# Layer 2 of a four-layer kernel in a new order, and pauses between the scatters of layer 0

## The chip, the cores and the metric

One core of one Trainium2 chip runs the whole program in one launch. The metric is the device time of an execution in microseconds.

## The reference

The input `x` is 16 batches of 128 tokens of 256 values. Four layers follow, each an attention and an FFN, added to `x` behind a gate `tanh(g)`. Only two parts matter here.

Layer 0's FFN is a shared FFN of 704 hidden values for all tokens and eight experts of 176, of which each token takes its best two:

```python
s1 = xf @ shared_fc1.T; s2 = xf @ shared_fc2.T
shared = silu(s1) * s2 @ shared_proj.T
top_p, top_i = top_k(softmax(xf @ gate_w.T), 2)
y = sum over the two experts of top_p * expert(xf) + sigmoid(xf @ shared_gate_w.T) * shared
```

Layer 2 is an attention to a context (16 heads of 16, scores clipped to +-50) and an FFN with values rounded to 8 bits and ternary weights:

```python
probs = softmax(clip(mask(clip(q @ k.T / 4))))
delta = rs * ((probs @ v) @ Wo.T + bo)
x = x + tanh(g_xattn[2]) * ((delta - mean) / sqrt(var + 1e-5) * gamma + beta)
act_quant(a) = round(a * 127 / max|a|) / (127 / max|a|)
gate = silu(act_quant(n) @ quant(w_gate).T); up = act_quant(n) @ quant(w_up).T    # n = layernorm(x)
x = x + tanh(g_ffn[2]) * (act_quant(gate * up) @ quant(w_down).T)
```

## The kernel before, in words

Each engine has a queue of instructions written out by hand: `pe_program`, `dve_program`, `act_program`, `pool_program`, `sp_program` of each stage. An engine runs its queue in order; a wait holds everything behind it. Marks are semaphores: `.up()` counts one, `.at(n)` waits for the n-th.

**Layer 0's FFN (`l0_ffn`).** The shared FFN is cut into 24 up blocks and 24 down blocks, v = 0 to 23 (four groups of batches, six pieces of the hidden width). For each: `pe_up` (L1052, eight matmuls), ScalarE's tanh (L1243), two multiplications on VectorE (L1187, L1189), `pe_down` (L1064). Blocks up to 17 (`LATE` is 18) run before the experts, the rest after them. When the routing is known (L1175), GpSimd scatters the tokens' rows to DRAM, 16 DMAs for each of the two choices (`pool_scatter`, L1265), and then gathers the first eight tiles' expert weights (L1485); the last two of these wait for up block 17. SyncE loads the sorted rows (L1523) when all scatters have landed. Then 39 tiles of 128 rows go through the experts (`pe_tile_up`, L1329, and so on).

**Layer 2 (`layer_2`).** A loop over 16 batches works on several at once: in iteration i the keys or queries of a pair are made two pairs ahead, the scores and exponentials of batch i, the attention result of batch i - 2 = y (sum and FFN up projection), and the FFN's hidden values and down projection of batch i - 3 = f. A batch's 16 heads are two units of eight, u = 2b and 2b + 1. Per unit: scores (L2653, eight matmuls), exponential on ScalarE (L3054), clip on VectorE (L2849), weighing of the values (`pe_weigh`, L2670), and `dve_normalise`: transpose (L2857), reciprocal (L2859), multiply (L2861), transpose back (L2866). The weights V hold a column of ones, so the sum of the probabilities comes with the product. Both units use the same 256 columns of one PSUM bank, `av_bank`; the output projection (`pe_project_out`, L2679, L2681) writes the same columns too.

On VectorE then: statistics of the projection (`dve_delta_stats`, L2871 to L2875), a scaling (L2879) and the sum into `x` (L2883), the FFN's layer norm statistics (L178 to L182), the rounding of the normalised values (`dve_ffn_quantise`, L2895 to L2904), and in `dve_ffn_gate` (L2914 to L2928) the product of gate and up, its maximum, three one-column steps for the scale and the rounding of 832 columns. The hidden values are transposed (`pe_turn_hq`, L2712), copied by ScalarE (L3078, L3079) and go through the down projection (L2719). GpSimd makes the root of every variance (`ln_root`, L190; `pool_delta_root`, L3174), splits projections into bf16 parts (L3165, L3169), makes scales (L3181, L3182, L3189), adds the FFN output (L3193), and in every odd iteration up to the ninth norms a pair of batches that comes three pairs later (L190 twice, L3147 twice, L3160 twice).

Functions named `ahead` are the start of layer 3, put into the last iterations.

## Time and profile before

| | |
|---|---|
| Runs | 1975.53 us median of 3 (1969.91 to 1983.47) |
| Profiled execution | 1976.86 us, span 1975.5 us |
| Busy in the span | PE 87%, DVE 67%, ACT 48%, POOL 40% |
| Mean granted clock of TensorE | 0.944 |

The profile is of one execution. PE is TensorE's matmuls, PEld its weight loads, DVE VectorE, ACT ScalarE, POOL GpSimd, SP SyncE. Times in it count from the start of the span. A row of a timeline merges like instructions that follow each other (x8 is eight of them); what stands in brackets is how long the engine sat idle before it and what released it. A window's row gives the busy time of each engine in a stretch.

### The profile page before, as it was taken

The page shows a single profiled execution, that of the slowest core. Times are in us where ns is not written, and L with a number is a line of the kernel's source. Part 1 is how long each engine was busy: PE and PEld are TensorE (multiplying, and loading weights), DVE is VectorE, ACT ScalarE, POOL GpSimd, SP SyncE. Part 2 cuts the span into 40 slices and gives each one's busy share as a digit, 9 for nine tenths or more (in the row PEclk, how much of TensorE's full clock was granted, in tenths as well). Part 3 has the DMA queues.
Part 4 walks back from the last instruction along what each step waited for, and adds up shares of the span by engine and source line. Part 5 has one row for each costly group of instructions (what it writes and reads, how often), then busy time and mean ns, then how long its engine had stood idle before and what let it go on. Part 6 is the DMA issues. An engine that isn't in the chain of part 4 may idle for free.

```text
span 1975.5 us, 35976 instructions
## 1 busy us (share of the span) xinstructions
PE 1726.9 (87%) x12221; PEld 1186.7 (60%) x12221; DVE 1330.4 (67%) x4195; ACT 942.1 (48%) x2227; POOL 790.8 (40%) x957
## 2 busy tenths in 40 slices
PE   6888888959897898998896787788999999988998
PEld 2444444636665777777685555455777777766445
DVE  8888873613356887887747888864576676666446
ACT  2666664203323777777644555323444444443352
POOL 3333321264664566564525454211124334433340
PEclk7999999979998999999998899788999999999899
DMA  4444422146963343443123443009100000030767
GB/s 109 102 121 101 95 55 71 36 164 218 299 182 86 82 93 78 87 92 78 32 77 95 145 125 87 18 1 308 46 18 36 32 8 4 13 97 15 232 213 306
DMA packets 180437, 200.41 MB, mean 101 GB/s; under 512 B 86500, under 2 KB 150129, under 8 KB 176928
## 3 DMA queue, kind: packets, MB, share of 16 engines
q1 hardware_dynamic: 161920, 155.92, 29.0%
q0 software_dynamic: 15168, 41.54, 6.2%
q8 instruction: 99, 1.62, 0.4%
q10 hardware_dynamic: 3168, 0.66, 0.2%
q14 instruction: 82, 0.67, 0.1%
HBM read 131.88 MB, written 75.44 MB: 105 GB/s over the span
## 4 chain that ended last, share of the span: by engine, by line
PE 51%; DVE 20%; ACT 10%; issue 7%; POOL 4%; DMA 3%; another core or an unknown queue 2%; ACTq 1%; SPq 1%; DVEq 0%; POOLq 0%
PE psum L3392 3%; PE psum L1052 3%; PE psum L389 3%; PE psum L3466 3%; PE psum L1329 2%; DVE sbuf L539 2%; PE psum L3441 2%; PE psum L352 2%; ACT sbuf L3829 2%; PE psum L3459 2%; PE psum L2278 2%; PE psum L1348 2%; PE psum L1064 2%; PE psum L1764 1%
## 5 line engine op out<-in xcount | busy, mean ns | idle before, releaser
L539 DVE TENSOR_REDUCE sbuf<-psum 128x2 f32<-128x512 f32 x256 | 164.8, 685 | 34.7 <-PE psum L352 33.7
L190 POOL TENSOR_TENSOR sbuf<-sbuf 128x1 f32<-128x1 f32 x128 | 73.5, 576 | 273.4 <-DVE sbuf L182 273.1
L2013 ACT ACTIVATE sbuf<-psum 128x512 f32<-128x512 f32 x256 | 138.4, 594 | 71.6 <-PE psum L1764 67.1
L3829 ACT ACTIVATE sbuf<-psum,sbuf 128x128 f32<-128x128 f32 x256 | 113.7, 455 | 89.2 <-DVE sbuf L3641 89.1
L681 ACT ACTIVATE sbuf<-psum 128x1024 f32<-128x1024 f32 x128 | 130.4, 1021 | 37.5 <-PE psum L374 30.0
L3921 POOL DMA_INDIRECT l_slot_inputs<-sbuf x96 | 97.3, 1014 | 100.7 <-DVE sbuf L3712 75.7
L3466 PE MATMUL psum<-sbuf 128*128 128x256 f32 x512 | 123.8, 385 | 4.9 <-DVE sbuf L3659 4.9
L3392 PE MATMUL psum<-sbuf 128*128 128x256 f32 x512 | 119.4, 388 | 0.8 <-ACT sbuf L3793 0.8
L352 PE MATMUL psum<-sbuf 112*128 112x256 bf16 x512 | 104.0, 288 | 13.1 <-DVE sbuf L539 7.8
L1889 DVE CUSTOM_DVE_ANT_0 sbuf<-psum,sbuf 128x128 f32<-128x128 f32 x512 | 112.5, 284 | 0.5 <-PE psum L1743 0.5
L3392 PEld LDWEIGHTS psum<-sbuf 128*128 128x128 f32 x512 | 98.7, 195 | 21.5 <-issue 8.8
L3466 PEld LDWEIGHTS psum<-sbuf 128*128 128x128 f32 x512 | 93.6, 193 | 16.1 <-issue 5.8
L1897 DVE TENSOR_REDUCE sbuf<-psum 128x8 f32<-128x1024 f32 x64 | 77.5, 1211 | 31.4 <-PE psum L1755 31.3
L352 PEld LDWEIGHTS psum<-sbuf 112*128 112x128 bf16 x512 | 41.6, 102 | 91.6 <-DVE sbuf L539 53.0
L1052 PE MATMUL psum<-sbuf 128*128 128x512 f32 (+1 forms) x192 | 88.0, 602 | 0.0
L3599 DVE COPY sbuf<-psum 128x1024 f32<-128x1024 f32 x32 | 39.2, 1224 | 65.0 <-ACT sbuf L3800 44.8
L2005 ACT ACTIVATE sbuf<-sbuf 128x128 f32<-128x128 f32 x256 | 81.4, 398 | 0.0
L3837 ACT ACTIVATE sbuf<-psum 128x512 f32<-128x512 f32 x64 | 38.4, 600 | 84.4 <-PE psum L3449 84.0
L374 PE MATMUL psum<-sbuf 128*128 128x512 bf16 x256 | 78.1, 387 | 0.3 <-ACT sbuf L681 0.2
L3459 PE MATMUL psum<-sbuf 128*128 128x512 f32 x128 | 69.3, 623 | 9.8 <-ACT sbuf L3837 9.8
L3441 PEld LDWEIGHTS psum<-sbuf 128*128 128x128 f32 x512 | 65.8, 195 | 17.3 <-issue 15.1
L1764 PE MATMUL psum<-sbuf 128*128 128x128 f32 x512 | 70.5, 281 | 5.2 <-ACT sbuf L2013 5.0
(436 smaller groups left out, 4501.5 us busy)
## 6 DMA issues: line engine op xcount, KB each, us to landing
l_pair_outputs<-sbuf SPq DMA_DIRECT2D x24, 512.0 KB, 7.0
sbuf<-in_l_gu_pairs SPq DMA_DIRECT2D x32, 384.0 KB, 8.6
sbuf<-l_pair_outputs SPq DMA_DIRECT2D x16, 768.0 KB, 15.9
sbuf<-l_q_parts SPq DMA_DIRECT2D x16, 384.0 KB
l_q_parts<-sbuf SPq DMA_DIRECT2D x64, 96.0 KB, 2.3
sbuf<-l_q_parts SPq DMA_DIRECT2D x32, 192.0 KB
l_k_parts<-sbuf SPq DMA_DIRECT2D x64, 96.0 KB, 2.2
sbuf<-l_k_parts SPq DMA_DIRECT2D x32, 192.0 KB
```

The source lines that it names most:

```text
L352: last = pe.matmul(score_bank[v % 2][:, j * T0:(j + 1) * T0], q3[0:STACK + 48, h, c * P:(c + 1) * P], k3[0:STACK + 48, h // 4, :], start=T ...
L539: dve.tensor_reduce(top3[:, 2 * hp:2 * hp + 2, c], score_bank[v % 2].rearrange("p (j t) -> p j t", j=2), AXX, ALU.max, negate=True).then_i ...
L681: act.activation(e_t[u % 12], shift_bank[u % 2], ACT.Exp).then_inc(*exped.up())
L1052: last = pe.matmul(up_bank[v % 2][0:M, n * BANK:(n + 1) * BANK], wn[:, k, fs], xt_t[blk][:, k, :], start=(k == 0), stop=(k == KD - 1))
L1889: last = dve.tensor_tensor_reduce(d_t[n % 3][:, head], self_bank[:, head], mask, -1.0, -LOWEST, ALU.add, ALU.min, mx[:, j:j + 1])
L2013: act.activation(e_t[i % 4][:, h * BANK:(h + 1) * BANK], turn_bank[:, h * BANK:(h + 1) * BANK], ACT.Exp).then_inc(*exped.up())
L3392: last = pe.matmul(q_bank[:, j * N:(j + 1) * N], w.wq[:, k, (4 * g + j) * P:(4 * g + j + 1) * P], xt_t[pair % 2][:, k, :], start=(k == 0), ...
L3441: last = pe.matmul(score_bank[:, j * P:(j + 1) * P], q[:, 4 * g + j, i * P:(i + 1) * P], kT_t[b % 3][:, g * P:(g + 1) * P], start=True, st ...
L3459: pe.matmul(av_bank, v_t[b % 3][:, g * P:(g + 1) * P], eT_t[u % 2], start=True, stop=True).then_inc(*valued.up())
L3466: last = pe.matmul(out_bank[:, 0:D], o_t[b % 2][:, h * P:(h + 1) * P], w.wo[:, h, :], start=(h == 0), stop=(h == H3 - 1))
L3829: last = act.activation(e_t[u % 3][:, j * P:(j + 1) * P], score_bank[:, j * P:(j + 1) * P], ACT.Exp, bias=mt[:, j:j + 1], scale=rq[:, lo + ...
L3921: pool.indirect_dma_start(out=route.x_slots[:, :], out_offset=bass.IndirectOffsetOnAxis(ap=route.slot[b][:, k:k + 1], axis=0), in_=xr_t[b ...
```

## The change

In layer 2:

- Both units of a batch are weighed in one go (16 matmuls over all 512 columns of the bank) and normalised in one go; the order of the heads in the packed result changes, and with it the rows of the output weights, which are laid out on the host (`by_group`).
- The order of the queues changes. The output projection of batch i - 1 comes late in iteration i instead of at the head of iteration i + 1. VectorE begins with the delta statistics; the clip, the attention sum and the FFN statistics follow, and only then the gate.
- The rounding of the hidden values moves from VectorE to ScalarE (`act_round_h`), in front of ScalarE's copies of the transposed values.
- The epsilon of each layer norm is no longer added by VectorE but by GpSimd, in front of the root.

In layer 0 GpSimd waits before every fourth scatter (but the first) for one more up block, 11 to 17.

```diff
+def ln_stats_only(m, src, n, var_ready, ring):
+    dve, chain, s = m.nc.vector, m.chain, ring[n % len(ring)]
+    dve.bn_stats(s[:, 0:6], src).then_inc(*chain.up())
+    dve.wait_ge(*chain.now())
+    dve.bn_aggr(s[:, 6:8], s[:, 0:6]).then_inc(*var_ready.up())
+
+def ln_root_of_variance(m, n, var_ready, eps_added, rstd_ready, ring):
+    pool, s = m.nc.gpsimd, ring[n % len(ring)]
+    pool.wait_ge(*var_ready.at(n + 1))
+    pool.tensor_scalar(s[:, 8:9], s[:, 7:8], EPS_LN, None, ALU.add).then_inc(*eps_added.up())
+    pool.wait_ge(*eps_added.now())
+    pool.tensor_tensor(s[:, 8:9], s[:, 8:9], m.half_neg, ALU.pow).then_inc(*rstd_ready.up())
...
             for b in range(NB):
+                if b % 4 == 0 and (k or b):
+                    pool.wait_ge(*upped.at(LATE - 7 + 4 * k + b // 4))
                 pool_scatter(b, k)
...
+    def pe_weigh(b):
+        pe.wait_ge(*clipped.at(2 * b + 2))
+        pe.wait_ge(*v_ready.at(b + 1))
+        if b:
             pe.wait_ge(*x_mid.at(b))
...
     def pe_project_out(b):
-        pe.wait_ge(*normed.at(2 * b + 2))
-        pe.wait_ge(*av_read.at(min(2 * b + 3, 2 * NB)))
+        pe.wait_ge(*normed.at(b + 1))
...
         for i in range(NB):                       # pe_program
             f, y, paired = i - 3, i - 2, made_in(i) < 2 * NPAIR
-            if y >= 0:
-                pe_project_out(y)
...
-            if f >= 0:
-                pe_turn_hq(f)
             if i + 2 < NB:
                 pe_values(i + 2)
             if i:
-                pe_weigh(2 * i - 1)
+                pe_weigh(i - 1)
+            if f >= 0:
+                pe_turn_hq(f)
+            if y >= 0:
+                pe_turn_xq(y)
             if f >= 0:
                 pe_down(f)
-            pe_weigh(2 * i)
-            if y >= 0:
-                pe_turn_xq(y)
             if i + 1 < NB:
                 pe_scores(2 * i + 2)
+            if i:
+                pe_project_out(i - 1)
             if y >= 0:
                 pe_up(y)
...
-        dve.tensor_scalar(c(9), c(8), c(5), 127.0, ALU.mult, ALU.mult).then_inc(*chain.up())
-        dve.wait_ge(*chain.now())
-        dve.tensor_scalar(h, h, c(9), ROUND, ALU.mult, ALU.add).then_inc(*h_round.up())
+        dve.tensor_scalar(c(9), c(8), c(5), 127.0, ALU.mult, ALU.mult).then_inc(*h_scaled.up())
...
         for i in range(NB):                       # dve_program
             f, y = i - 3, i - 2
-            if i % 2 == 1:
-                dve_clip(2 * i)
+            if y >= 0:
+                dve_delta_stats(y)
+            dve_clip(2 * i)
+            if y >= 0:
+                dve_add_attention(y)
+                dve_ffn_stats(y)
             if f >= 0:
                 dve_ffn_gate(f)
             if y >= 0:
-                dve_delta_stats(y)
-            if i % 2 == 0:
-                dve_clip(2 * i)
-            if y >= 0:
-                dve_add_attention(y)
-                dve_ffn_stats(y)
+                dve_ffn_quantise(y)
             if i:
-                dve_normalise(2 * i - 1)
-            if y >= 0:
-                dve_ffn_quantise(y)
+                dve_normalise(i - 1)
             dve_clip(2 * i + 1)
-            dve_normalise(2 * i)
...
+    def act_round_h(f):
+        act.wait_ge(*h_scaled.at(f + 1))
+        act.activation(h_t[f % 2], h_t[f % 2], ACT.Identity, bias=plus_round, scale=s_t[f % 3][:, 9:10]).then_inc(*h_round.up())
...
     def pool_delta_root(b):
-        s = y_t[b % 2][:, 8:9]
+        s = y_t[b % 2]
         pool.wait_ge(*y_var.at(b + 1))
-        pool.tensor_tensor(s, s, m.half_neg, ALU.pow).then_inc(*y_rstd.up())
+        pool.tensor_scalar(s[:, 8:9], s[:, 7:8], EPS_LN, None, ALU.add).then_inc(*eps_added.up())
+        pool.wait_ge(*eps_added.now())
+        pool.tensor_tensor(s[:, 8:9], s[:, 8:9], m.half_neg, ALU.pow).then_inc(*y_rstd.up())
```

## Rows read from the trace of the kernel before

**Rows 1.** Page, part 4, then the chain from 380 to 470 us: start, length, what.

```profile
PE 51%; DVE 20%; ACT 10%; issue 7%; POOL 4%; DMA 3%; another core or an unknown queue 2%; ACTq 1%; SPq 1%; DVEq 0%; POOLq 0%
...
403.03 17.91 another core or an unknown queue
...
420.99 19.62 another core or an unknown queue
```

**Rows 2.** Timeline of PE, 380 to 480 us: start, length, line, operation, forms, idle before.

```profile
404.54 3.60 PE L1052 MATMUL psum<-sbuf 128*128 128x512 f32 x8
...
409.70 3.60 PE L1052 MATMUL psum<-sbuf 128*128 128x512 f32 x8
...
455.85 1.45 PE L1329 MATMUL psum<-sbuf 128*128 128x352 f32 x4 [0.26 <-ACT sbuf L1441]
```

**Rows 3.** Timeline of POOL from 150 us on and from 405 us on.

```profile
387.14 1.21 POOL L1265 DMA_INDIRECT l_slot_inputs<-sbuf  x1 [33.19 <-DVE sbuf L1175]
...
428.31 1.01 POOL L1485 DMA_INDIRECT sbuf<-in_l_expert_rows,sbuf  x1 [0.30 <-issue]
```

**Rows 4.** Windows of layer 0: length; busy PE, PEld, DVE, ACT, POOL; clock; DMA; GB/s.

```profile
435.00:440.00 5.00, 0.00 (x0) 0.00 (x0) 0.00 (x0) 0.00 (x0) 0.55 (x1) 0.50 0.98 381
```

**Rows 5.** Windows, two batches of layer 2, same columns.

```profile
1152.95:1180.57 27.62, 21.58 (x185) 14.82 (x185) 24.97 (x67) 16.33 (x27) 15.33 (x22) 1.00 0.47 126
```

**Rows 6.** Timeline of DVE, 1152 to 1181 us.

```profile
1169.71 1.02 DVE L2914 SCALAR_TENSOR_TENSOR sbuf<-sbuf,psum 128x832 f32<-128x832 f32 x1
...
1173.71 0.77 DVE L2928 TENSOR_SCALAR sbuf<-sbuf 128x832 f32<-128x832 f32 x1
1174.40 0.42 DVE L2871 BATCH_NORM_STATS2 sbuf<-psum 128x6 f32<-128x256 f32 x1
...
1175.14 0.68 DVE L2849 TENSOR_SCALAR sbuf<-sbuf 128x1024 f32<-128x1024 f32 x1
1175.74 0.49 DVE L2879 SCALAR_TENSOR_TENSOR psum<-psum,sbuf 128x256 f32<-128x256 f32 x1
1176.36 0.48 DVE L2883 SCALAR_TENSOR_TENSOR sbuf<-psum,sbuf 128x256 f32<-128x256 f32 x1
...
1177.69 0.45 DVE L2857 STREAM_TRANSPOSE sbuf<-psum 128x256 f32<-128x256 f32 x1
...
1178.98 0.38 DVE L2895 TENSOR_REDUCE sbuf<-sbuf 128x1 f32<-128x256 f32 x1
```

**Rows 7.** Timeline of ACT, 1152 to 1181 us.

```profile
1161.69 0.90 ACT L3078 ACTIVATE sbuf<-psum,sbuf 128x768 bf16<-128x768 f32 x1
1162.49 0.35 ACT L3079 ACTIVATE sbuf<-psum,sbuf 64x128 bf16<-64x128 f32 x1
```

**Rows 8.** Timeline of PE, 1150 to 1200 us.

```profile
1155.46 0.69 PE L2679 MATMUL psum<-sbuf 1*128 1x256 f32 x2
1156.09 1.13 PE L2681 MATMUL psum<-sbuf 128*128 128x256 f32 x4
...
1158.78 0.61 PE L2653 MATMUL psum<-sbuf 96*128 96x128 bf16 x8
1160.67 0.98 PE L2712 MATMUL psum<-sbuf 128*128 128x128 f32 x7 [1.27 <-DVE sbuf L2928]
...
1163.23 1.06 PE L2719 MATMUL psum<-sbuf 128*128 128x256 bf16 x7
```

**Rows 9.** Timeline of POOL, 1152 to 1181 us.

```profile
1153.52 0.34 POOL L3182 TENSOR_SCALAR sbuf<-sbuf 128x1 f32<-128x1 f32 x1
...
1169.12 0.55 POOL L190 TENSOR_TENSOR sbuf<-sbuf 128x1 f32<-128x1 f32 x1 [1.29 <-DVE sbuf L182]
...
1170.40 2.44 POOL L3147 TENSOR_SCALAR sbuf<-sbuf 128x256 f32<-128x256 f32 x2
1172.80 1.23 POOL L3160 TENSOR_TENSOR sbuf<-sbuf 128x256 f32<-128x256 f32 x2
1175.31 0.94 POOL L3174 TENSOR_TENSOR sbuf<-sbuf 128x1 f32<-128x1 f32 x1 [1.27 <-DVE sbuf L2875]
```

105 lines of the change are left out of this document (49 added, 56 removed).

## The prediction

> **What bounds the kernel now.** I read the page for its share of busy time first, then the chain of waits for two stretches, then each engine's timeline there. The diff touches two places that have nothing to do with each other: the scatters of layer 0 and the loop of layer 2.
>
> In layer 0 the chain shows one odd thing [rows 1]: from 403.03 to 420.94 and from 420.99 to 440.61 us the path is "another core or an unknown queue", 37.5 us in which no engine is the cause; the page gives this item 2% of the whole span, so there is no second such place. The timelines say what it is. TensorE finishes up block 14 at 404.54 + 3.60 = 408.14 and block 15 at 409.70 + 3.60 = 413.3 [rows 2]. ScalarE's tanh of block 14 waits for nothing else that is open, yet starts at about 420.96, the end of the first piece in the chain, and that of block 15 at 440.63, the end of the second. TensorE's signal for finished work arrives 12.8 and 27.3 us late. During all this GpSimd issues 32 scatters with no pause (387.14 to 428.31, one every 1.29 us) and then, still with no pause, weight gathers [rows 3]. The experts' first projection starts only at 455.85 [rows 2], while their input rows and weights have been on their way since 428 to 430.
>
> In layer 2 two batches take 27.62 us, 13.81 each, with VectorE busy 24.97 of it, TensorE 21.58, ScalarE 16.33, GpSimd 15.33, TensorE's clock at 1.00 [rows 5]. VectorE is the bound: its queue has nearly no hole, and TensorE waits for it before the transposes of the hidden values (1.27 us [rows 8]).
>
> **The change part by part, layer 0.** The new waits let the scatters go four at a time: the first four at once, each further four when up block 11, 12, ... 17 is done. Four scatters take 4 x 1.29 = 5.15 us; TensorE does one up and one down block in 409.70 - 404.54 = 5.16 us [rows 2]. So if signals come in time the waits cost 0.1 us each. Block 17 would be done at 413.3 + 2 x 5.3 = 423.9, the last four scatters end at 429.0 instead of 428.3: +0.7 us. Behind GpSimd's waits are queued the gathers of the expert weights; behind the last scatter SyncE's loads of the rows. Nobody else uses GpSimd here.
>
> What they can buy: signals are late only inside this stream of 38 DMA issues in a row. Later gathers and stores, and layer 3's scatters, show no such piece (the 2% are used up). A pause could let the signal pass; the trace has no pause in the stretch, so nothing shows it. Bounds: 0 gained, or all of it. If all, the shared blocks end near 428 and the experts' start is set by their data: two gathers are issued by 431.6; all six and the first rows, some 4.5 MB, need 12 us at the 381 GB/s of [rows 4]. A start is possible between 434 and 443; the first pair needs a third of the data, so I take 437: 455.85 - 437 = **18.8 us gained**, between 13 and 22.
>
> Beside this a rule of the Trainium skill. By the row, the signal of block 14 is acted on 12.8 us after the last matmul's modelled end. "TensorE: Matmul & The Clock Gate", section "The mechanism", says that matmuls end in strict order and that one increment on the last is sound; it knows no lateness, and by it alone ScalarE would have started at 408. The row decides.
>
> **Layer 2, what VectorE loses.** Per batch: the rounding, 1174.40 - 1173.71 = 0.69 us [rows 6]; the epsilon after the delta statistics, of 0.74 us (1174.40 to 1175.14) about 0.18 (its own 0.07 and the wait for the aggregation, estimated), since the next instruction no longer waits for that; as much after the FFN statistics and half a time two in the norm statistics: 0.6 in all. One normalised unit takes 1.29 us (1177.69 to 1178.98), two 2.6; one double one I put at 1.9 (a transpose of 128x512 for 0.45, estimated at 0.72; reciprocal 0.24; multiply 0.45; transpose 0.45): 0.7 saved. Together 2.0 us of 13.8. ScalarE gains one pass over 832 columns, about 0.9 us (768 columns take 0.90 [rows 7]), and has 5 us free per batch. GpSimd gains three or four additions of one column. No row has one; 0.2 below (a free-running one) and 0.6 above (0.34 for a like instruction [rows 9] and its wait). I take 0.38, nearest to the 0.34.
>
> **What is late next.** Fewer VectorE cycles help only if VectorE stays the bound, and the new order closes a loop. Delta statistics of a batch now head VectorE's iteration, and wait for an output projection that TensorE runs after the down projection and the scores. The gate is behind the attention sum. So, from one end of a projection to the next: signal 0.05; delta statistics 0.56; clip 0.60 (1175.14 to 1175.74); scale 0.62 with its wait (to 1176.36); attention sum and FFN statistics 1.33 - 0.25 = 1.08 (1176.36 to 1177.69 less the epsilon); gate down to its scale 3.95 (1169.71 to just before 1173.71) [rows 6]; ScalarE's rounding 0.95; seven transposes 1.04; ScalarE's two copies 1.19; down 1.0; scores 0.58; projection 1.76 (1155.46 to 1157.22) [rows 7, 8]. Sum **13.4 us**, against 13.81 now. Of VectorE's 2.0 us only 0.4 arrives; the rest turns into VectorE waiting for the projection. TensorE, 10.8 us of work per batch [rows 5], fits in.
>
> **GpSimd's pair work.** In odd iterations up to the ninth it does, for a later pair: two roots, 1170.40 - 1169.12 = 1.28 us, now 2.05 with two additions; the norm of two batches 2.44; beta 1.23 [rows 9]. This is ahead of the next batch's delta root in its queue. Now this costs nothing: VectorE's gate (4 us) runs between, and GpSimd idles 1.27 us before that root at 1175.31. In the new order that cover is gone: the delta statistics come right after the projection. GpSimd starts the block when its addition of the FFN output is done, about 0.47 (ScalarE's scaling of 256 columns, between its 0.35 and 0.90 [rows 7]) + 0.7 (GpSimd's 0.62, half of beta, and its start) + 0.1 = 1.3 us after the down projection, which is 1.0 us before the projection's end T. It ends the block at T - 1.0 + 5.7 = T + 4.7, the root with its addition is there at T + 5.7; VectorE needs it at T + 1.83. So 3.9 us are lost once in two iterations (3.2 to 4.7 for the bounds of the addition). Two batches: 2 x 13.4 + 3.9 = 30.7 against 27.6, +3.1. It happens at iterations 1, 3, 5, 7, 9; the first lies in the start-up, where VectorE is full of weight rounding: 4 x 3.1 = +12.4. After iteration 9 the 0.4 of a batch come back, about -1; TensorE, with holes of 4 us, may be granted less than 1.00 for a while, +2. Layer 2: **+13 us**, bounds -2 and +20.
>
> A rule of the Trainium skill here: VectorE's multiply and GpSimd collide. "SBUF — State Buffer", section "Who interferes with whom", calls the shared port pair an exclusive lock. By it the bigger multiply, if it meets the norm block, would wait out one of its instructions (1.2 us); it stands in VectorE's spare time by the sum above, so I leave it at nothing.
>
> **Sum.** 1976.9 (the profiled execution; its span is 1975.5) - 18.8 + 13 = 1971; that execution is 1.3 above the median, so 1970 us.
>
> **Rivals.** *(1) The GpSimd block is hidden and the loop is shorter than summed*, because the projection overlaps more or roots come earlier: layer 2 gains 0.4 to 1.5 us in each of 13 batches, -5 to -20. For it: VectorE does lose 2.0 us. Against it: the queue order, in the diff. With layer 0's gain 1937 to 1952. *(2) Slower: the signals stay late.* Then GpSimd itself waits for the late signal, which it did not before, and scatters, row loads and gathers, all queued behind, move with it. Last scatter: issued after block 17's signal, about 441 + 5 instead of 428, experts' data some 8 us later, start near 461: +5. Decisive is whether the four-wise pause lets the signals through. 1976.9 - 1.3 + 13 + 5 = 1994, to 2000. For it: the second late signal came at 440.61, 12 us after the last scatter [rows 1, 3], so the end of the scatters alone did not free it. Against it: less is queued if scatters stop early. *(3) The stall belongs to ScalarE*: it is not GpSimd's stream that holds it but something of its own that comes late either way. Layer 0 then gives 0: 1989. By the Trainium skill's "Runtime: NRT & Kernel Launch", section "Instruction fetch mechanics", an engine's code comes in blocks over its own DMA queue and is mostly hidden; no row here shows ScalarE short of code.
>
> **Chances.** Forecast 0.44 (1960 to 1982); (1) 0.25; (2) 0.18; (3) 0.13. The measurement of this kernel tells about 1% (20 us) from no change. Faster by over 1% needs both (1) and the gain of layer 0, or the forecast's lower edge: 0.28. Slower by over 1%: most of (2) and the upper edge of (3): 0.19. Within 1%: 0.53. The range, to hold it 8 times in 10, leaves out the lower half of (1) and the end of (2): 1948 to 1996.
>
> **What would show it.** In layer 0: no piece of an unknown queue in the chain, tanh of blocks 14 to 17 about 5.2 us apart, gaps of 0.1 to 0.4 us after every fourth scatter, the experts' first projection near 437. In layer 2: two batches in about 30.7 us, 13.4 and 17.3 in turn; VectorE's attention sum waiting for GpSimd's root in even iterations and GpSimd without idle time before it; VectorE busy about 21 us per two batches; ScalarE's rounding followed at once by the transposes. I am wrong if the period falls under 13 us or the root is never waited for, or if the late signals are still there.

## The result, and the profile after

The changed kernel takes 2004.16 us (median of 4 runs, 1996.22 to 2008.68) against 1974.36 (4 runs, 1969.91 to 1983.47) for the kernel before on the same chip: ratio 1.0133, 95% interval 1.0102 to 1.0164. It is slower by 1.3%; I had forecast 1970, with a range of 1948 to 1996. The profiled execution of after took 2008.68 us, its span is 2007.3, so it stands 31.8 us above the profiled execution of before.

Where the 31.8 us arise, read from the start times of the same line in both traces: the experts' last down projection of layer 0 starts 7.6 us earlier than before (557.5 against 565.1), the first scores of layer 2 start 2.4 us earlier, layer 3's first projection of its loop starts 27.3 us later (1317.5 against 1290.2), the end is 31.8 later. Layer 0 gained, and 34 us were lost from the entry of layer 2 on.

Page of after, part 1:

```profile
PE 1736.1 (86%) x12191; PEld 1195.5 (60%) x12221; DVE 1296.8 (65%) x4068; ACT 958.4 (48%) x2243; POOL 799.1 (40%) x1005
```

**Layer 0.** Timeline of POOL: the scatter behind the only late signal that is left, and the last scatter.

```profile
419.31 0.97 POOL L1282 DMA_INDIRECT l_slot_inputs<-sbuf  x1 [2.90 <-remote]
...
433.36 0.97 POOL L1282 DMA_INDIRECT l_slot_inputs<-sbuf  x1 [0.30 <-issue]
```

Timeline of ACT and then of PE in the same stretch:

```profile
410.80 0.60 ACT L1260 ACTIVATE sbuf<-psum 128x512 f32<-128x512 f32 x1 [4.56 <-PE psum L1069]
418.56 0.60 ACT L1260 ACTIVATE sbuf<-psum 128x512 f32<-128x512 f32 x1 [7.17 <-remote]
```

```profile
440.36 1.12 PE L1336 MATMUL psum<-sbuf 128*128 128x128 f32 x4 [9.87 <-issue]
444.08 2.69 PE L1348 MATMUL psum<-sbuf 128*128 128x352 f32 x4 [2.60 <-issue]
```

Of the two late pieces of 17.91 and 19.62 us [rows 1] one is left, of 7.17 us with the tanh's own regular wait of 4.56 in it. GpSimd's next group of scatters waited 2.90 us for it, TensorE had no hole there; the experts' first up projection starts at 444.08 instead of 455.85 [rows 2].

**Layer 2.** Window of two batches, with the columns of [rows 5]:

```profile
1153.86:1189.26 35.40, 25.80 (x186) 17.47 (x186) 21.42 (x52) 18.41 (x29) 16.56 (x28) 0.84 0.37 97
```

VectorE does 21.42 us of work where it did 24.97 [rows 5], and the two batches take 35.40 us where they took 27.62. TensorE has no more to compute, but is busy 25.80 us instead of 21.58: the granted clock has gone from 1.00 to 0.84. The timelines of VectorE, GpSimd, ScalarE and TensorE say how:

```profile
1161.25 0.43 DVE L2882 BATCH_NORM_STATS2 sbuf<-psum 128x6 f32<-128x256 f32 x1 [5.83 <-PE psum L2696]
...
1175.85 0.43 DVE L2882 BATCH_NORM_STATS2 sbuf<-psum 128x6 f32<-128x256 f32 x1 [1.69 <-PE psum L2696]
...
1181.50 0.48 DVE L2893 SCALAR_TENSOR_TENSOR sbuf<-psum,sbuf 128x256 f32<-128x256 f32 x1 [4.02 <-POOL sbuf L3188]
```

```profile
1174.22 0.72 POOL L3207 TENSOR_TENSOR sbuf<-sbuf 128x256 f32<-128x256 f32 x1 [2.97 <-ACT sbuf L3094]
...
1176.61 2.80 POOL L3159 TENSOR_SCALAR sbuf<-sbuf 128x256 f32<-128x256 f32 x2
1179.38 1.23 POOL L3172 TENSOR_TENSOR sbuf<-sbuf 128x256 f32<-128x256 f32 x2
...
1180.90 0.57 POOL L3188 TENSOR_TENSOR sbuf<-sbuf 128x1 f32<-128x1 f32 x1
```

```profile
1186.57 1.08 ACT L3079 ACTIVATE sbuf<-sbuf 128x832 f32<-128x832 f32 x1 [1.99 <-DVE sbuf L2936]
```

```profile
1170.30 0.98 PE L2727 MATMUL psum<-sbuf 128*128 128x128 f32 x7 [1.77 <-ACT sbuf L3079]
...
1172.52 1.06 PE L2734 MATMUL psum<-sbuf 128*128 128x256 bf16 x7 [1.02 <-ACT sbuf L3087]
...
1174.68 1.13 PE L2696 MATMUL psum<-sbuf 128*128 128x256 f32 x4
...
1187.71 1.75 PE L2727 MATMUL psum<-sbuf 128*128 128x128 f32 x7 [3.44 <-ACT sbuf L3079]
...
1190.70 1.78 PE L2734 MATMUL psum<-sbuf 128*128 128x256 bf16 x7 [0.81 <-ACT sbuf L3087]
...
1194.53 2.08 PE L2696 MATMUL psum<-sbuf 128*128 128x256 f32 x4
```

Follow the second batch. GpSimd's pair block (1174.91 to 1180.6) is ahead of the delta root in its queue; the attention sum waits 4.02 us for it. So the gate is 4 us late, the rounding is, and TensorE stands idle 3.44 us before the transposes of the hidden values. The same seven transposes then take 1.75 us instead of 0.98, the down projection 1.78 instead of 1.06, the projection's second part 2.08 instead of 1.13: TensorE has dropped from 2.4 to 1.2 GHz. VectorE waits 6.20 us for the projection that follows at 1196.65, where the cycle of the first batch had it wait 1.69.

The starts of the delta statistics, one a batch, in the two traces: from the third to the eleventh, four pairs of batches, before takes 113.96 us and after 142.20 (+28.2); from the entry of layer 2 to the third after is 8.7 us faster; from the eleventh to the sixteenth 90.81 against 73.79 (+17.0). The first and the last of these numbers hold a shift of the mark itself, since the new order puts the delta statistics at the head of VectorE's iteration. Counted by the transposes of the hidden values, of which the first start 47.5 us behind the entry before and 47.7 after, it is +0.2 to the first, +7.6 to the third, +21.8 to the eleventh, +7.7 to the last.

**The end of layer 2.** The queue behind the loop has a new order too; VectorE's, as a cut:

```diff
-        dve_ffn_gate(NB - 3)
         dve_delta_stats(NB - 2)
         ahead.dve_keep_queries(0, 0)
         dve_add_attention(NB - 2)
         dve_ffn_stats(NB - 2)
-        dve_normalise(2 * NB - 1)
+        dve_ffn_gate(NB - 3)
```

`keep_queries` copies a projection of layer 3. Timelines of VectorE and of TensorE after, then of VectorE before:

```profile
1322.24 1.23 DVE L3613 COPY sbuf<-psum 128x1024 f32<-128x1024 f32 x1 [8.50 <-ACT sbuf L3814]
...
1325.08 1.01 DVE L2924 SCALAR_TENSOR_TENSOR sbuf<-sbuf,psum 128x832 f32<-128x832 f32 x1
```

```profile
1330.20 1.76 PE L2727 MATMUL psum<-sbuf 128*128 128x128 f32 x7 [3.63 <-ACT sbuf L3079]
```

```profile
1285.06 1.02 DVE L2914 SCALAR_TENSOR_TENSOR sbuf<-sbuf,psum 128x832 f32<-128x832 f32 x1 [1.14 <-ACT sbuf L3071]
...
1297.18 1.23 DVE L3599 COPY sbuf<-psum 128x1024 f32<-128x1024 f32 x1 [6.72 <-ACT sbuf L3800]
```

VectorE waits for layer 3's projection in both, but before it has done the gate by then; after, the gate stands behind the wait, and with it the rounding, the transposes and all that follows.

### The profile page after: what moved, and what is told of

Its sections match the earlier page's. It is cut to its first block and busy times, and to the rows that moved or that the text cites. A ratio compares the mean times of both kernels' runs of the same rounds, so it can differ in the third digit from the quotient of the medians.

```text
span 2007.3 us, 35853 instructions
## 1 busy us (share of the span) xinstructions
PE 1736.1 (86%) x12191; PEld 1195.5 (60%) x12221; DVE 1296.8 (65%) x4068; ACT 958.4 (48%) x2243; POOL 799.1 (40%) x1005
## 5 line engine op out<-in xcount | busy, mean ns | idle before, releaser
L207 POOL TENSOR_TENSOR sbuf<-sbuf 128x1 f32<-128x1 f32 x96 | 53.9, 564 | 241.5 <-DVE sbuf L182 241.2
L1916 DVE TENSOR_REDUCE sbuf<-psum 128x8 f32<-128x1024 f32 x64 | 77.5, 1212 | 33.7 <-PE psum L1774 33.5
L391 PE MATMUL psum<-sbuf 128*128 128x512 bf16 x226 | 71.2, 386 | 2.4 <-ACT sbuf L698 0.5
## 6 DMA issues: line engine op xcount, KB each, us to landing
sbuf<-l_pair_outputs SPq DMA_DIRECT2D x16, 768.0 KB, 15.1
```

## The experiments

Five series; in each the kernel before ran on the same chip. "Two batches" is a window from one delta statistics to the second next, where the pair work of iterations 3 to 9 goes on. "Layer 2" is the time from the start of its first scores to the start of its last transpose of hidden values: 277.2 us in before, 314.3 in after; in a second trace of before (before_again, below) 270.4, which is the better measure where there are no late signals. A dummy matmul counts twice in the traces, as every fp32 matmul of this form does.

**First series: the two halves, and two repairs of after.** The kernel before took 1940.63 us here (13 runs), 34 less than in the comparison above.

l0_waits_only, the kernel before with

```diff
             for b in range(NB):
+                if b % 4 == 0 and (k or b):
+                    pool.wait_ge(*upped.at(LATE - 7 + 4 * k + b // 4))
                 pool_scatter(b, k)
```

> The kernel before with nothing but the waits between the scatters. Theory A (late signals come from the unbroken stream of scatters, and the waits in layer 0 are worth what the two traces differ by there): in the changed kernel's trace the experts' last down projection starts 7.7 us earlier although that trace lost 2.6 us before the first scatter, so 10 us gained: 1974.4 - 10 = 1964 us, one short piece of an unknown queue (about 3 us) in place of two of 18 and 20. Theory B (the two changes act on each other, or the 10 us are chance of one execution): 1974 us, and the long pieces are back.

Measured: 1946.79 us (10 runs), ratio 1.0031 (1.0000 to 1.0062). No late signal is in the trace, and so the waits had nothing to gain. Neither theory was put to the test.

l2_only, the kernel after without these two lines.

> The changed kernel without the waits between the scatters. Theory A (layer 2 alone costs the 36 us by which the two traces drift apart from 1050 to 1370 us; layer 0 goes back to two late signals): 1974.4 + 36 = 2010 us, up to 2014. Theory B (layer 2 costs less and part of the loss is from elsewhere): under 2004 us, that is, not slower than the changed kernel.

Measured: 1985.28 us, ratio 1.0215 (1.0149 to 1.0282); layer 2 takes 317.9 us. Windows of l2_only:

```profile
1139.92:1176.12 36.20, 28.10 (x185) 18.65 (x184) 21.07 (x51) 18.42 (x29) 16.70 (x28) 0.78 0.26 66
```

Theory A's place holds: all of the loss is in layer 2 (44.7 us against the 36 that it said, over a before that is 34 lower). No late signal in this trace either, though nothing interrupts its scatters: whether signals come late is not a matter of the kernel alone.

pool_block_moved, the kernel after with GpSimd's roots and norm of a pair ahead of its addition, its betas one iteration later, and VectorE's statistics for them one iteration earlier:

```diff
-            if i % 2 == 1 and i // 2 + 3 < NPAIR:
+            if i % 2 == 0 and i // 2 + 3 < NPAIR:
                 dve_norm_stats(i // 2 + 3)
...
             if y >= 0:
                 pool_scales(y)
+            if i % 2 == 1 and pair < NPAIR:
+                pool_roots(pair)
+                pool_norm(pair)
+            if i % 2 == 0 and i and pair - 1 < NPAIR:
+                for n in range(PAIR * (pair - 1), PAIR * pair):
+                    pool_add_beta(n)
             if f >= 0:
                 pool_add_out(f)
```

> The changed kernel with GpSimd's pair work taken out of the way: VectorE makes the pair's norm statistics one iteration earlier, GpSimd's roots and norm of the pair stand before the addition of the FFN output of the odd iteration, the betas in the next one. Theory A (the block stands before the delta root; it holds VectorE 4.0 us in five iterations, and the hole it makes costs TensorE its clock for the rest of that cycle, 3.4 us more): 2004 - 5 x 7.4 = 1967 us; cycles of about 14 us in all iterations, clock near 1.00. Theory B (the block costs only its wait; the clock falls for the low load anyway): 2004 - 20 = 1984 us, cycles of 14 and 17 us still alternate in clock. Theory C (the wait moves to another engine): within 5 us of 2004.

Measured: 1973.56 us, ratio 1.0156 (1.0091 to 1.0221); layer 2 takes 299.6. Windows, and VectorE's timeline:

```profile
1147.65:1178.15 30.50, 22.79 (x186) 15.62 (x185) 21.57 (x51) 18.31 (x29) 16.65 (x29) 0.94 0.32 79
```

```profile
1165.53 0.48 DVE L2893 SCALAR_TENSOR_TENSOR sbuf<-psum,sbuf 128x256 f32<-128x256 f32 x1 [0.36 <-POOL sbuf L3188]
```

The wait for the root is gone (0.36 instead of 4.02), and with the hole the clock is back to 0.94. It takes 18 us off the 318 of layer 2 in l2_only; before has 270. The kernel itself is 11.7 us below l2_only, which is short of both theories (37 and 20 us below after, which did not run on this chip).

pe_kept_busy, the kernel after with dummy matmuls ahead of the transposes of the hidden values (their result is read by nobody):

```diff
                 pe_weigh(i - 1)
+            if f >= 0 and i + 2 < NB:
+                pe_keep_busy(i + 2, 3 if i % 2 else 6)
             if f >= 0:
                 pe_turn_hq(f)
...
+    def pe_keep_busy(b, n):
+        pe.wait_ge(*v_ready.at(b + 1))
+        for _ in range(n):
+            pe.matmul(pro_bank[:, 0:D], m.ctxT[:, 0, 0:S], w.wv[:, 0, :], start=True, stop=True)
```

> The changed kernel with matmuls nobody reads put into TensorE's queue where it waits for ScalarE's rounding (six of 128x256 in even iterations, three in odd ones, into the projection bank while it is free; only added work, results untouched). Theory A (the hole of 3.4 us in even iterations is what makes the granted clock fall, and transposes, down projection, scores and output projection at the lower clock cost 3.4 us per pair): the granted clock in the loop goes from 0.84 to near 1.00, even cycles from 20.8 to about 17.4 us, 2004 - 17 = 1987 us or a little less. Theory B (the clock falls for another reason): clock stays at 0.84, 2004 us or more, since the additional work can only hold TensorE up.

Measured: 1971.83 us, ratio 1.0148 (1.0086 to 1.0209); layer 2 takes 297.0. Windows, VectorE's and TensorE's timeline:

```profile
1155.04:1186.21 31.17, 25.39 (x204) 18.25 (x203) 20.69 (x50) 18.53 (x29) 16.70 (x29) 1.00 0.30 77
```

```profile
1160.69 0.48 DVE L2900 SCALAR_TENSOR_TENSOR sbuf<-psum,sbuf 128x256 f32<-128x256 f32 x1 [4.02 <-POOL sbuf L3195]
```

```profile
1166.89 0.98 PE L2727 MATMUL psum<-sbuf 128*128 128x128 f32 x7 [0.65 <-ACT sbuf L3086]
```

Theory A (the kernel is 13.4 us below l2_only), and the cleanest separation of the study: the wait for the root is as long as ever (4.02), TensorE runs at 1.00, and two batches take 31.17 us, where my sum without a clock loss said 30.7. Against after (35.40) and l2_only (36.20) the clock costs 4.2 to 5.0 us of two batches.

**Second series: both repairs, more repairs, and two parts in the old order.** The kernel before 1938.79 us (7 runs).

before_again, the kernel before, one run.

> The kernel before, unchanged, for a profile of it on this chip. If the late TensorE signals of layer 0 are a property of the kernel, its trace has the same two pieces (about 12 and 27 us of GpSimd-side lateness, the experts' first up projection at about 456 us). If they belong to the chip or the session, the trace has none, the experts' first up projection starts at about 437 us, and the span is near 1940 us. Layer 2, from its first weigh to its last down projection, about 272 to 277 us.

Measured: 1939.91 us, span 1938.6, layer 2 270.4. Timeline of ACT, the tanh of the block that was 27.3 us late in the first comparison, and of PE, the experts' first up projection:

```profile
414.83 0.60 ACT L1243 ACTIVATE sbuf<-psum 128x512 f32<-128x512 f32 x1 [4.56 <-PE psum L1052]
```

```profile
438.39 2.68 PE L1329 MATMUL psum<-sbuf 128*128 128x352 f32 x4 [2.16 <-issue]
```

Same kernel, no lateness, the experts' first up projection at 438.39 instead of 455.85 [rows 2], their last down projection at 537.2 instead of 565.1: the late signals are of the chip or the session, and they cost 28 us of the 1975. Another 6.8 us are in layer 2, most of them at its end: VectorE's wait for layer 3's projection is 1.96 us here and 6.72 in the first trace, where that projection (L3392, 16 matmuls) took 5.88 us instead of 3.69, partly at the lower clock. (My 437 for a start without lateness was good.)

moved_and_busy, pool_block_moved and pe_kept_busy in one.

> The kernel after with both earlier edits at once: GpSimd's pair block moved ahead of its add, and TensorE kept busy with dummy matmuls. Theory A (two separate causes, the late delta root and the clock, about 18 to 20 us each): layer 2 takes 274 to 282 us and the time is within 0.5% of the kernel before. Theory B (one cause, a hole on TensorE which either edit closes): no better than each alone, layer 2 at 295 to 300 us, the time 1.2 to 1.6% above before.

Measured: 1966.66 us, ratio 1.0122 (1.0080 to 1.0165), layer 2 296.3. Windows, and VectorE's timeline:

```profile
1133.72:1164.03 30.31, 25.17 (x204) 18.34 (x203) 21.19 (x51) 18.45 (x29) 16.82 (x28) 1.00 0.33 88
```

```profile
1164.03 0.43 DVE L2889 BATCH_NORM_STATS2 sbuf<-psum 128x6 f32<-128x256 f32 x1 [2.81 <-PE psum L2696]
```

The time and layer 2 are those of theory B, though two batches are shorter than with either repair; they are 2.7 us above before. With full clock and no wait for a root, VectorE still waits 2.81 us for each projection. That was the loop of my 13.4 us, one of the two cycles at 13.75 and the other 16.55. The repairs alone don't bring the time back, and most of what is left lies elsewhere: of the 26 us by which layer 2 is longer than in before_again, 10 are there at the eleventh transposes of hidden values, and 16 come behind them. VectorE's wait for layer 3's projection, with the gate behind it, is 7.52 us here.

short_and_busy, this with scores and output projection ahead of the down projection, and ScalarE's exp ahead of its scale:

```diff
-            if f >= 0:
-                pe_down(f)
             if i + 1 < NB:
                 pe_scores(2 * i + 2)
             if i:
                 pe_project_out(i - 1)
+            if f >= 0:
+                pe_down(f)
```

> As moved_and_busy, and with TensorE's scores and output projection ahead of the down projection and ScalarE's second exp ahead of its scale. If the loop is still set by the chain scores, exp, clip, weigh, normalise, projection, it takes 0.5 to 1 us off each iteration, 8 to 15 us off layer 2, and the kernel is 0.3 to 0.8% faster than before. If VectorE's own work (about 12.1 us a batch) or ScalarE's sets it, nothing comes of it: within 0.2% of moved_and_busy.

Measured: 1960.28 us, ratio 1.0104 (1.0055 to 1.0153), layer 2 286.7: some 10 us less in layer 2, but the ratio is not told from that of moved_and_busy, and is far from the 0.3 to 0.8% below before that a shorter chain was to give. Windows:

```profile
1178.09:1207.96 29.87, 25.01 (x204) 18.46 (x203) 20.55 (x47) 18.11 (x29) 13.44 (x23) 1.00 0.32 80
```

Its better cycles are 13.75 us again, and the timeline shows a second loop: from the delta statistics to the last transpose of the normalisation VectorE works through everything it has (11.9 us, 1.5 of it a wait for the delta root), and the projection, 1.8 us long, can only then start. In the new order VectorE has only one clip left to do beside it, and waits 1.26 us.

parts_old_order, the kernel before with the epsilons on GpSimd and the rounding on ScalarE, nothing else.

> The kernel before with only two parts of the change: the epsilons on GpSimd and the rounding on ScalarE, in the old order and with each unit normalised by itself. VectorE loses 4 small instructions and the rounding per batch (about 1.0 us), GpSimd gains about 0.5 us a batch, ScalarE 1.07 us. Theory A (the joint weighing and the new order are what costs): within 0.5% of before, layer 2 at 268 to 280 us. Theory B (the rounding on ScalarE or the epsilons on GpSimd lie on the loop's chain): layer 2 gains 8 to 15 us, the time is 0.4 to 0.8% above before.

Measured: 1965.69 us, ratio 1.0122 (1.0078 to 1.0166), layer 2 297.4. Theory A fell: these two parts alone, in the old order, cost as much as everything together after a repair.

**Third series: one part each.** The kernel before 1973.28 us (13 runs); here the three kernels without waits between scatters have two late signals each again (36.4, 36.4 and 36.6 us of wait on ScalarE).

round_old_order, the kernel before with the rounding on ScalarE:

```diff
-        dve.tensor_scalar(c(9), c(8), c(5), 127.0, ALU.mult, ALU.mult).then_inc(*chain.up())
-        dve.wait_ge(*chain.now())
-        dve.tensor_scalar(h, h, c(9), ROUND, ALU.mult, ALU.add).then_inc(*h_round.up())
+        dve.tensor_scalar(c(9), c(8), c(5), 127.0, ALU.mult, ALU.mult).then_inc(*h_scaled.up())
...
+            if f >= 0:
+                act_round_h(f)
             act_exp(2 * i + 1)
```

> The kernel before with the rounding on ScalarE alone. Both together (rounding and epsilons) cost 1.2% and took layer 2 from 270 to 297 us. Theory A (the rounding is the cost: TensorE's transposes of the hidden values stand ahead of its weighing, and VectorE waits for the weighing behind ScalarE's 1.07 us): 0.8 to 1.2% above before, VectorE waiting 1 to 3 us for the weighing in each iteration. Theory B (the epsilons are the cost): within 0.3% of before.

Measured: 1996.15 us, ratio 1.0118 (1.0076 to 1.0159), layer 2 294.6. Windows, VectorE's timeline, TensorE's timeline:

```profile
1154.11:1188.65 34.54, 26.06 (x187) 17.50 (x184) 25.03 (x65) 18.47 (x30) 15.32 (x23) 0.85 0.37 99
```

```profile
1177.60 0.45 DVE L2858 STREAM_TRANSPOSE sbuf<-psum 128x256 f32<-128x256 f32 x1 [3.33 <-PE psum L2670]
```

```profile
1173.47 1.52 PE L2712 MATMUL psum<-sbuf 128*128 128x128 f32 x7 [2.12 <-ACT sbuf L3074]
1174.79 1.91 PE L2639 MATMUL psum<-sbuf 128*128 128x256 f32 x4
1176.63 0.88 PE L2670 MATMUL psum<-sbuf 128*32 128x128 f32 x16
```

The rounding's 1.07 us on ScalarE stands between the gate and the transposes; in TensorE's queue values and weighing stand behind these; VectorE waits for the weighing. TensorE's hole before the transposes grows from 1.27 [rows 8] to 2.12 us, and behind it values take 1.91 us instead of some 1.1. A move of 0.69 us of work off the bound engine costs 23 us. This is theory A, with a wait of VectorE (3.33 us) a little above the 1 to 3 that it named.

eps_old_order, the kernel before with the epsilons on GpSimd:

```diff
+    dve.bn_aggr(s[:, 6:8], s[:, 0:6]).then_inc(*var_ready.up())
...
+    pool.tensor_scalar(s[:, 8:9], s[:, 7:8], EPS_LN, None, ALU.add).then_inc(*eps_added.up())
+    pool.wait_ge(*eps_added.now())
```

> The kernel before with the epsilons on GpSimd alone. Theory A (as above, the rounding is the cost): within 0.3% of before, layer 2 at 265 to 275 us. Theory B (the epsilons are: each root comes 0.4 us later, four of them a batch, on the path to the attention sum and to the quantised rows): 0.5 to 1.2% above before, VectorE waiting for the root.

Measured: 1969.54 us (10 runs), ratio 0.9964 (0.9937 to 0.9991), layer 2 268.5. Windows:

```profile
1149.88:1177.36 27.48, 21.67 (x184) 14.82 (x184) 24.23 (x62) 16.47 (x28) 17.10 (x29) 1.00 0.47 125
```

This part is harmless: VectorE's work falls by 0.7 us in two batches, the two batches by 0.14. Its trace has both late signals (ScalarE waits 18.07 and 18.37 us), and its last down projection of the experts starts at 565.0, so the 0.36% are not from a signal that came in time.

joint_old_order, the kernel before with both units weighed and normalised together. It leaves out the new head order of the output projection's weights, so what it projects is another mix of heads; its work is the same.

```diff
             if i:
-                pe_weigh(2 * i - 1)
+                pe_weigh(i - 1)
             if f >= 0:
                 pe_down(f)
-            pe_weigh(2 * i)
...
             if i:
-                dve_normalise(2 * i - 1)
+                dve_normalise(i - 1)
             if y >= 0:
                 dve_ffn_quantise(y)
             dve_clip(2 * i + 1)
-            dve_normalise(2 * i)
```

> The kernel before with one part of the change alone: both units of a batch weighed and normalised together; the rounding, the epsilons and the order of the queues stay as before, and there are no waits between scatters. In the old order VectorE has no hole, so its 13.8 us a batch should fall by what the joint normalisation saves. Theory A (VectorE is the bound in the old order, and the change lost its gain by its order and by the rounding): 0.4 to 0.7 us off a batch, layer 2 at 265 to 272 us, the time 0.2 to 0.6% below before. Theory B (the joint weighing is itself a cost, because the second unit now waits a whole iteration and the projection comes later): layer 2 gains 5 us or more, the time is 0.3% above before or more.

Measured: 1995.37 us, ratio 1.0115 (1.0079 to 1.0151), layer 2 292.9. Theory A fell. Windows, VectorE's timeline, TensorE's timeline:

```profile
1136.05:1170.41 34.36, 25.82 (x184) 17.42 (x184) 24.27 (x59) 16.56 (x28) 15.24 (x22) 0.85 0.48 130
```

```profile
1158.12 0.72 DVE L2849 STREAM_TRANSPOSE sbuf<-psum 128x512 f32<-128x512 f32 x1 [3.36 <-PE psum L2667]
...
1164.70 0.69 DVE L2844 TENSOR_SCALAR sbuf<-sbuf 128x1024 f32<-128x1024 f32 x1 [2.27 <-ACT sbuf L3045]
```

```profile
1161.88 0.69 PE L2691 MATMUL psum<-sbuf 128*128 128x128 f32 x2 [2.84 <-DVE sbuf L2896]
1162.36 1.06 PE L2653 MATMUL psum<-sbuf 96*128 96x128 bf16 x8
```

Before, TensorE's timeline:

```profile
1152.95 0.44 PE L2695 MATMUL psum<-sbuf 128*128 128x128 f32 x2 [1.38 <-DVE sbuf L2904]
```

The joint step saves VectorE 0.7 us in two batches and takes away what filled two holes: TensorE's second weighing stood behind the down projection, VectorE's second normalisation between the quantised rows and the gate. Now TensorE idles 2.84 us there, where before it idled 1.38, scores take 1.06 us instead of 0.61, exp and tanh are late, VectorE waits for both.

gate_first, the kernel after with the gate ahead of the delta statistics, and the up projection ahead of the output projection:

```diff
+            if f >= 0:
+                dve_ffn_gate(f)
             if y >= 0:
                 dve_delta_stats(y)
             dve_clip(2 * i)
             if y >= 0:
                 dve_add_attention(y)
                 dve_ffn_stats(y)
-            if f >= 0:
-                dve_ffn_gate(f)
```

> The kernel after with the gate put back ahead of the delta statistics on VectorE, and TensorE's up projection ahead of its output projection so that the gate has its input. Theory A (the gate behind the attention sum is what uncovered GpSimd's pair block and closed the loop of 13.75 us in which all of VectorE's work and the projection follow one another): the two-batch period falls from 35 to 28 to 30 us, layer 2 to 275 to 288 us, the time 0.3 to 1.0% above before. Theory B (the rounding on ScalarE and the clock it costs set the time whatever the order): layer 2 stays above 295 us, the time 1.3% above before or more.

Measured: 1995.47 us, ratio 1.0103 (1.0056 to 1.0151), with the waits between scatters gaining some 13 us here (below), layer 2 311.0. Windows, VectorE's timeline:

```profile
1148.71:1184.30 35.59, 28.12 (x184) 18.77 (x184) 21.46 (x51) 18.32 (x30) 16.45 (x28) 0.76 0.27 67
```

```profile
1180.41 1.02 DVE L2924 SCALAR_TENSOR_TENSOR sbuf<-sbuf,psum 128x832 f32<-128x832 f32 x1 [4.33 <-ACT sbuf L3075]
```

The cover for GpSimd's block is back (0.36 us of wait), and the 4 us are spent waiting for ScalarE's tanh instead. Theory B holds for layer 2; that the time is only 1.0% above before is owed to the waits.

**Fourth series: the clock in the two parts that cost, the best repair, and the waits again.** The kernel before 1944.35 us (13 runs).

round_and_busy, round_old_order with `pe_keep_busy(i + 2, 7)` behind `pe_weigh(2 * i)`.

> round_old_order (1.18% above before, two batches 34.5 us at a clock of 0.85) with seven dummy matmuls on TensorE where it waits about 2 us for VectorE's quantised rows. Theory A (the clock is the main cost, the rounding itself costs little): granted clock 0.95 to 1.00 in the pair part of layer 2, two batches 28.5 to 31 us, the time within 0.6% of before. Theory B (ScalarE's 1.07 us in the chain is the cost): two batches stay above 33 us, 1.0% above before or more.

Measured: 1971.59 us, ratio 1.0148 (1.0093 to 1.0203). Windows:

```profile
1139.49:1173.02 33.53, 29.12 (x212) 20.80 (x212) 24.28 (x66) 18.26 (x29) 15.43 (x22) 0.95 0.28 72
```

Theory B by the number, but the filling was too long (3.29 us in a hole of 2) and stood behind the other hole, which it left at 2.11 us. It decides nothing.

joint_and_busy, joint_old_order with the new head order and `pe_keep_busy(i + 2, 8)` behind `pe_down(f)`.

> joint_old_order (1.15% above before, two batches 34.4 us at a clock of 0.85) with eight dummy matmuls behind the down projection, where TensorE waits 2.8 us for the quantised rows. Theory A (clock): 0.95 to 1.00, scores and up projection of even iterations back to 0.61 and 1.57 us, two batches 28.5 to 31 us, the time within 0.6% of before. Theory B (the wait for the joint weighing, 3.4 us on VectorE in even iterations, is the cost by itself): two batches 32 us or more, 0.9% above before or more.

Measured: 1965.12 us, ratio 1.0112 (1.0052 to 1.0172), layer 2 286.0. Windows:

```profile
1143.51:1174.44 30.93, 28.22 (x216) 20.99 (x216) 24.60 (x59) 16.44 (x28) 15.26 (x22) 1.00 0.32 78
```

Clock and two batches as theory A said, the time as theory B: eight dummies take 3.72 us, about 1 us too long in each iteration.

round_back_short, the kernel after with the rounding back on VectorE, GpSimd's block moved and the short order on TensorE, without dummies.

> The kernel after with the rounding back on VectorE, GpSimd's pair block moved ahead of its add, and on TensorE the scores and the output projection ahead of the down projection (ScalarE's exp ahead of its scale). VectorE does 12.6 us a batch and then waits 1.8 us for the projection. Theory A (the new order itself is a closed loop of VectorE's whole work and one projection): 14.2 to 14.6 us a batch, layer 2 at 278 to 290 us, 0.2 to 0.8% above before. Theory B (the rounding was what kept this order from paying): 13.3 us a batch or less, at or below before.

Measured: 1972.99 us, ratio 1.0149 (1.0094 to 1.0204), layer 2 302.1, two batches 33.7 us at a clock of 0.85. Worse than both theories: without dummies TensorE has holes of 0.5 to 1.6 us at four or five places of an iteration, and is granted 0.85 though no one of them is long.

l0_waits_again, l0_waits_only once more.

> The kernel before with the waits between scatters alone, measured once where no late signal showed (ratio 1.0031, within the measurement). If this chip shows late signals in kernels without waits (time of before near 1973 us): layer 0 ends 8 to 14 us earlier and the time is 0.4 to 0.7% below before. If it shows none (before near 1940): within 0.4% of before, as the first time.

Measured: 1948.44 us (10 runs), ratio 1.0021 (0.9991 to 1.0052), no late signal. The waits alone met no chip with lateness. What they do there is seen in the third series: the experts' last down projection starts at 552.4 in gate_first, which has them, and at 565.0, 566.2 and 566.8 in the three that don't.

**Last series.** The kernel before 1939.98 us (20 runs).

joint_half_filled, joint_and_busy with 4 dummies for 8.

> As joint_and_busy, with four dummy matmuls instead of eight (1.86 us in a hole of 2.8 to 3.2 us, so they delay nothing). Theory A (the clock is the main cost of the joint weighing in the old order): clock 0.95 to 1.00 in the pair part, two batches 28 to 29.5 us, the time within 0.4% of before. Theory B (the waits are costly by themselves, at any clock): clock up, yet two batches 30.5 to 31.5 us, 0.8 to 1.1% above before. Theory C (so few do not hold the clock): clock 0.85 to 0.90, two batches 33 us or more.

Measured: 1953.44 us (9 runs), ratio 1.0054 (1.0035 to 1.0074), layer 2 282.1. Windows, TensorE's timeline:

```profile
1152.67:1183.15 30.48, 25.20 (x200) 17.78 (x200) 24.64 (x59) 16.44 (x28) 15.26 (x22) 1.00 0.31 80
```

```profile
1157.32 1.99 PE L2721 MATMUL psum<-sbuf 128*128 128x256 f32 x8
1160.57 0.44 PE L2691 MATMUL psum<-sbuf 128*128 128x128 f32 x2 [1.25 <-DVE sbuf L2903]
1160.84 0.61 PE L2653 MATMUL psum<-sbuf 96*128 96x128 bf16 x8
```

Between theories A and B. Dummies that delay nothing halve the cost (1.0115 on another chip to 1.0054, intervals apart). Of the 6.7 us that the joint step adds to two batches about 3.9 are clock and 2.9 the wait itself. It is shown here most directly that a kernel becomes faster by useless work.

waits_and_eps, l0_waits_only and eps_old_order in one.

> The kernel before with the waits between the scatters and the epsilons on GpSimd, the two parts that cost nothing by themselves. On a chip without late signals (before near 1940) within 0.3% of before; with late signals (before near 1973) 0.4 to 0.9% below before. Rival: the epsilons' 0.36% of gain came from the late signal that this kernel happened to lose in layer 0, then the parts do not add: 0.2 to 0.5% below before where there are late signals.

Measured: 1938.47 us (12 runs), ratio 0.9985 (0.9961 to 1.0008), layer 2 267.7. No late signal on this chip, so this run does not test the rival; the trace of eps_old_order, with both late signals in it, speaks against it. It has the lowest median of all changed kernels, and is not told from before.

## Why the prediction was wrong

**TensorE's clock: the step that failed.** I wrote "TensorE, with holes of 4 us, may be granted less than 1.00 for a while, +2". The hole was there as forecast (3.44 us), and the price was not 2 us in all but 3.4 us in the second cycle of every pair: 0.77 at the transposes, 0.72 at the down projection, 0.42 at the scores, 1.5 at the projection. pe_kept_busy shows it by taking only this away: 35.40 us fall to 31.17, 4.2 us in all. From the third to the eleventh delta statistics I had forecast 4 x 3.1 = 12.4 and measured 28.2, 15.8 more; four times 4.2 is 17, so the clock covers the difference. I priced a drop of the clock as an accident of a few us; here each hole repeats every pair of batches, so its price does too.

**The late root: right.** 3.9 us once in two iterations, by the order of GpSimd's queue: 4.02 measured in after, and 0.36 once the block is moved.

**The loop of 13.4 us: right in its members, and nearly in its size.** The cycle from 1161.25 to 1175.85 takes 14.6. ScalarE's rounding takes 1.07 for my 0.95 and stands in its queue behind an exponential, the centring of the next rows and the split of the projections, so the transposes start at 1170.30, 0.9 us later than the gate allows. Most of this is the clock again: with dummies the same cycle takes 13.76 (pe_kept_busy), and 13.75 with both repairs (moved_and_busy). So two batches: 30.7 forecast, + 0.5 for loop and root, + 4.2 for the clock = 35.4, measured 35.40.

**"VectorE is the bound": true and misleading.** I took from [rows 5] that the rounding and the joint step, as less work on VectorE, can only help or not matter, and asked of them only where their own work goes. The one-part runs show the old loop balanced to a fraction of a us: rounding +1.18%, joint step +1.15%, each while VectorE's work fell or stayed. Both lengthen a wait of TensorE (1.27 to 2.12 us, 1.38 to 2.84). For the joint step joint_half_filled shows that the clock makes more than half of the cost; for the rounding this is not shown. My bounds for layer 2, -2 and +20, had no case with a clock lost in every pair.

**The end of layer 2: a second step that failed.** "After iteration 9 the 0.4 of a batch come back, about -1": from the eleventh transposes of hidden values to the last the change costs 7.7 us, and 14.4 against before_again, where before has no lateness. Some 3 of these 14.4 are two cycles of 16.4 and 17.1 us instead of 15.1 and 15.2. The clock is low there (0.67), but it is 0.70 in before as well, so how much of the 3 is clock is not shown. The largest part is one gap, 25.1 us against 15.4 in before_again (21.1 in before, which has its own wait of 6.72 there). I had not looked at the queue behind the loop. In it the gate stands behind VectorE's wait for layer 3's projection: 8.50 us in after, 5.3 to 11.0 in all versions with the new order. In the old order the wait is 2.0 to 6.7 us, and the gate is ahead of it. This is read from the traces; no run puts the gate back.

**The start of layer 2** is no gain, though the third delta statistics come 8.7 us earlier: by the transposes of hidden values after is 0.2 us behind before at the first and 7.8 us at the third. I had put this stretch at nothing.

**Layer 0: right in kind, half the size.** The waits let the signals through, all but one, as forecast. The experts' projection starts at 444.08, in a trace whose first scatter is already 2.6 us later: 14.4 us gained there, and 10.2 at the experts' last down projection, for 18.8. Of these 5.2 are gone by the entry of layer 2; no run says why, and the four executions of before here differ by 13.6 us among themselves. On the chips that show no lateness the waits gain nothing: 0.3 and 0.2% slower were measured, each within or at the edge of its interval.

**The rivals.** Rival 1 (faster by a hidden block) fell with the 4.02 us. Rival 2 (signals stay late) and rival 3 (ScalarE's own stall) fell with the trace of after. The result lies above rival 2's number by another mechanism. The meeting of multiply and norm block that I had left at nothing is nothing in after: VectorE's joint multiply takes 0.42 us at 1171.60, while GpSimd is idle. So after doesn't test the lock. By the Trainium skill, "SBUF — State Buffer", section "Who interferes with whom", the two would exclude each other if they met. Another pair behaves so in round_old_order (last section).

**What stays open:** why signals come late on some chips or in some sessions; what the rounding alone costs at full clock (round_and_busy was badly filled); what the end of layer 2 would take with the gate ahead of the wait.

## What to carry to other kernels

In a loop like this one, look at TensorE's holes before you take work off the "bound" engine: two moves that lengthened a hole from 1.3 or 1.4 us to 2 or 3 in each round cost 7 us in two batches each, and with the joint step more than half of it was the clock, in the matmuls that follow. Ask of each removed or merged instruction what waits it was filling, and price a clock loss per round, not per kernel. Read the queue behind the loop as carefully as the loop: here one gap in it grew by 4 to 10 us. And profile the kernel before on the same chip as the change: 28 us of the 1975 here belonged to the chip or the session, not to the code.

## What the runs showed of the hardware

- TensorE went from 2.4 to 1.2 GHz behind holes of 2.1 us (transposes 1.52 us for 0.98), 2.8 us (scores 1.06 for 0.61) and 3.4 us (1.75 for 0.98); behind one of 1.77 us in after the transposes still took 0.98. The longest hole alone doesn't tell it: round_back_short, with several of up to 1.6 us, was granted 0.85, and in gate_first the values behind a hole of 1.58 us took 2.08 us instead of 1.13; before, with two of 1.3 to 1.4 us a batch, was granted 1.00. Four dummy matmuls (1.99 us) in a hole of 2.8 us held it at 1.00.
- ScalarE acted on TensorE's finished work 12.8 and 27.3 us late [rows 1, 2] while GpSimd issued scatters without a pause. The same two late waits are in the traces of two of six comparisons (before: 1974 and 1973 us), and in none of the other four (before: 1939 to 1944). Waits before every fourth scatter removed most of it (one wait of 7.2 us left in after and in gate_first, against two of 36.4 to 36.6 us in sum).
- In round_old_order VectorE's 128x128 multiply, 0.29 us where it is free, takes 1.10 us when GpSimd is in its subtraction, and ends 0.14 us behind it. In before it takes 0.57 us at 1154.12, and ends 0.15 us behind GpSimd's addition of 0.72 us at 1153.82 (timelines of round_old_order, of DVE and of POOL):

```profile
1178.32 1.10 DVE L2862 TENSOR_TENSOR sbuf<-sbuf 128x128 f32<-128x128 f32 x1
```

```profile
1178.12 1.16 POOL L3177 TENSOR_TENSOR sbuf<-sbuf 128x512 bf16<-128x512 f32 x1 [3.22 <-ACT sbuf L3040]
```

- Moving a pass of 832 columns from VectorE (0.69 us) to ScalarE (1.07 us) made it 0.4 us longer and added a crossing between engines.
